# The recurrence at the end of a hybrid attention kernel: 32x32 squares turned by VectorE, and the residual added by GpSimd

## The reference, cut to what matters

```
x = x + window_attention(group_norm(x))                  # layer 0
t = tokens(x)                                            # (16, 3136, 128)
t = t + linear_attention(layer_norm(t))
# the last part:
Wx = layer_norm(t) @ W.T ; Wx = batch_norm(Wx) * gamma + beta
def step(yt, wx_t):
    yt = sigmoid(wx_t + yt @ V.T)
    return yt, yt
ys = scan(step, 0, Wx over the 3136 time steps)          # for each of 16 images
out = t + ys
```

## Time and profile before

| | us |
|---|---|
| median of three runs (1854.69, 1854.74, 1855.60) | 1854.74 |
| span of the profiled execution | 1848.6 |
| what lies around the span, median less span | 6.1 |
| window attention up to about | 787 |
| linear attention, from there to about | 1565 |
| twelve warming steps | 1570.2 to 1585.3 |
| 196 kept steps | 1585.3 to 1840.9 |
| agreement test, last stores and end | 1840.9 to 1848.6 |

### The profile page before, as it was taken

One profiled execution on the slowest core, in us unless ns is written; L12 is line 12 of the kernel. 1 busy time (PEld: TensorE's weight loads), 2 busy tenths in 40 slices (PEclk: granted clock), 3 DMA queues, 4 the chain that ended last, 5 costly groups with the idle time before them and its releaser, 6 DMA issues.

```text
span 1848.6 us, 57765 instructions
## 1 busy us (share of the span) xinstructions
PE 1821.1 (99%) x19624; PEld 1615.1 (87%) x19624; DVE 1523.8 (82%) x4706; ACT 1214.1 (66%) x3179; POOL 1009.8 (55%) x1177
## 2 busy tenths in 40 slices
PE   7999999999999999899999999999999999999998
PEld 6888888888888888799999999999999998888886
DVE  7888888888888888788888888888888887566665
ACT  5777778877787877666666666666666665333333
POOL 6878888888888888633333333333333334432321
PEclk9999999999999999999999999999999999999999
DMA  5333333333333332122222222222223222656543
GB/s 169 102 104 107 107 107 105 105 103 103 105 107 107 107 85 80 47 70 74 66 69 68 67 68 67 70 65 70 64 70 91 70 68 74 222 183 218 190 166 127
DMA packets 207108, 187.02 MB, mean 101 GB/s; under 512 B 14576, under 2 KB 190944, under 8 KB 206816
## 3 DMA queue, kind: packets, MB, share of 16 engines
q1 hardware_dynamic: 205664, 182.14, 32.9%
q10 hardware_dynamic: 1152, 1.13, 0.2%
HBM read 105.95 MB, written 77.27 MB: 99 GB/s over the span
## 4 chain that ended last, share of the span: by engine, by line
PE 54%; issue 27%; POOL 16%; DVE 1%; DMA 1%; POOLq 0%; ACT 0%; ACTq 0%; DVEq 0%; SPq 0%
POOL la_rstd L999 11%; PE k_psum L346 7%; PE k_psum L296 6%; PE k_psum L289 6%; PE k_psum L314 6%; PE k_psum L330 5%; PE k_psum L362 5%; PE k_psum L1425 5%; PE k_psum L1416 5%; PE k_psum L280 4%; POOL la_spread L993 3%; PE k_psum L1406 2%; PE k_psum L1433 2%; POOL la_tn L1004 2%; POOLq L39 0%
## 5 line engine op out<-in xcount | busy, mean ns | idle before, releaser
L993 POOL TENSOR_SCALAR la_spread<-la_mv 128x4 f32<-128x4 f32 (+1 forms) x203 | 45.8, 226 | 477.9 <-DVE la_mv L1103 477.8
L615 POOL TENSOR_TENSOR wa_prob<-wa_prob,wa_peak 128x784 f32<-128x784 f32 x128 | 194.6, 1521 | 117.3 <-DVE wa_peak L481 117.3
L940 ACT ACTIVATE la_ve<-k_psum 128x256 f32<-128x256 f32 x196 | 75.4, 385 | 232.5 <-PE k_psum L821 232.5
L999 POOL TENSOR_TENSOR la_rstd<-la_spread,k_exponent 128x4 f32<-128x4 f32 (+1 forms) x203 | 207.5, 1022 | 17.2 <-POOL la_spread L993 0.4
L1490 ACT ACTIVATE sc_y<-k_psum,sc_cols 128x256 f32<-128x256 f32 x207 | 98.0, 473 | 177.0 <-PE k_psum L1425 177.0
L809 PE MATMUL k_psum<-la_uT,la_wt 128*128 128x256 f32 x784 | 201.9, 380 | 0.0
L622 POOL TENSOR_TENSOR wa_prob<-wa_prob,wa_inv 128x784 f32<-128x784 f32 x128 | 195.0, 1523 | 11.3 <-DVE wa_inv L442 11.3
L1059 DVE SCALAR_TENSOR_TENSOR la_fqk<-k_psum,la_raised 128x512 f32<-128x512 f32 x196 | 135.6, 692 | 74.8 <-ACT la_raised L932 74.6
L1214 POOL TENSOR_TENSOR sc_ub<-sc_tb 128x3584 f32<-128x3584 f32 (+6 forms) x22 | 92.8, 4222 | 172.6 <-PE k_psum L1406 171.3
L473 DVE TENSOR_TENSOR wa_prob<-k_psum,wa_bias 128x784 f32<-128x784 f32 x128 | 125.0, 976 | 66.2 <-PE k_psum L314 66.1
L932 ACT ACTIVATE la_raised<-k_psum,la_minus_one 128x512 f32<-128x512 f32 x196 | 134.7, 687 | 43.3 <-PE k_psum L809 43.1
(11 more groups left out here) (138 smaller groups left out, 5299.5 us busy)
## 6 DMA issues: line engine op xcount, KB each, us to landing
t<-la_tn SPq DMA_DIRECT2D x196, 129.0 KB, 2.2
la_xc<-x SPq DMA_DIRECT2D x196, 128.0 KB, 2.1
wa_xT<-in_x_cm SPq DMA_DIRECT2D x124, 196.0 KB, 3.3
sc_tb<-t SPq DMA_DIRECT2D x12, 1806.0 KB, 8.1
out<-sc_ob SPq DMA_DIRECT2D x12, 1792.0 KB, 12.1
wa_xw<-in_x_tok SPq DMA_DIRECT2D x64, 224.0 KB, 2.7
wa_xw<-in_x_tok SPq DMA_DIRECT2D x64, 168.0 KB, 2.3
x<-wa_y SPq DMA_DIRECT2D x64, 168.0 KB, 2.8
```

Of the source, the lines that this page charges most:

```text
L615: nc.gpsimd.tensor_tensor(s, s, peak[:, k % S, :].unsqueeze(2).broadcast_to([128, PAIRS * HEADS, WIN]), ALU.subtract).then_inc(lowered, 1)
L999: nc.gpsimd.tensor_tensor(rstd[:, n % S, used], spread[:, used], exponent[:, used], ALU.pow).then_inc(rooted, 1)
```

## The change

t2 gets another layout: (128, 196 steps, 8 blocks, 33). Partition p = 32 q + c holds channels 32 q to 32 q + 31 of the columns c, 32 + c, 64 + c, ..., and behind each 32 channels stands the reciprocal deviation. So a step's 128 x 256 numbers consist of 4 x 8 squares of 32x32, and turning each square in place puts channels on the partitions. VectorE does this, SBUF to SBUF, for two steps in one instruction. Linear attention writes the rows of `tn` in this layout: each token's row becomes four pieces of 33 numbers, and a store is cut wherever a segment ends. `tn` holds four pieces of 33.

In the scan, the two matmuls of a step are split into two halves of 128 columns, with semaphores and PSUM banks of their own. `uT` has four buffers of two steps, `y` three, `ob` three tiles. Most tiles have 10 steps for 14. The residual is added by GpSimd in one instruction for each tile, in place in `ob`; only for the last two tiles (4 and 2 steps) does VectorE do it. The output is written in the squares' layout and put in order on the host. Of the columns, 7 of 8 blocks are loaded early, for 3 of 4 half groups before.

```
-        EARLY = 3 * UNITS // 4
+        EARLY = -(-EARLY_BLOCKS * SQ * STEPS // (2 * P))
...
                     sp.wait_ge(tabled, n + 1)
-                    sp.dma_start(rows(t2, n), tn[:, n % XS]).then_inc(stored[n % XS], 16)
+                    for a, p, q, col, s in pieces(n):
+                        dst = bass.AP(t2.tensor, ((col % SQ * STEPS + s) * NB + col // SQ) * SF,
+                                      [[NB * SF, q - p], [SQ * STEPS * NB * SF, QUADS], [1, SF]])
+                        sp.dma_start(dst, tn[p:q, n % XS, a]).then_inc(stored[n % XS], 16)
...
+MAIN_PLAN = [(0, 4, True), (4, 8, True)] + [(12 + 10 * j, 10, True) for j in range(17)] + [(182, 8, True), (190, 4, True), (194, 2, True)]
+KEPT_TILES = 3
+U_PAIRS = 4
+Y_PAIRS = 3
+EARLY_BLOCKS = 7
...
+        for j in range(TILES + 4):
+            if inside(j - 4, TILES) and j - 4 >= FIRST:
+                store(j - 4)
+            if inside(j, TILES):
+                load(j)
...
+        def residual(j):
+            if not inside(j, TILES) or not by_pool(j):
+                return
+            pool.wait_ge(y_turned, pairs_to[j] + by_pool(j) - WARM_PAIRS)
+            size = 2 * by_pool(j)
+            kept = ob[:, slot(j), 0:size, :].rearrange("p s (b r) -> p s b r", b=NB)
+            nc.gpsimd.tensor_tensor(kept, kept, tb[:, j % 4, 0:size, :, 0:SQ], ALU.add).then_inc(pool_summed, 1)
+
+        for j in range(TILES + 2):
+            scale(j)
+            residual(j - 2)
...
+        for t in range(-1, NT):
+            for h in range(2):
+                state_part(t, h)
+                input_part(t + 1, h)
...
+        def turn_tokens(p):
+            if not inside(p, PAIRS):
+                return
+            j, i = where[p]
+            dve.wait_ge(u_made, j + 1)
+            at_least(dve, w_done, 4 * (p - U_PAIRS + 1))
+            nc.vector.transpose(uT[:, p % U_PAIRS].rearrange("p s c -> p (s c)"),
+                                ub[:, j % 2, i:i + 2].rearrange("p s b r -> p (s b r)")).then_inc(u_turned, 1)
...
+        def turn_states(p):
+            if not inside(p, PAIRS) or p < WARM_PAIRS:
+                return
+            j, i = where[p]
+            for h in range(2):
+                dve.wait_ge(y_made[h], 2 * p + 2)
+            at_least(dve, stored[slot(j)], stores(j))
+            states = y[:, p % Y_PAIRS].rearrange("p s c -> p (s c)")
+            if i < 2 * by_pool(j):
+                nc.vector.transpose(ob[:, slot(j), i:i + 2, :].rearrange("p s c -> p (s c)"), states).then_inc(y_turned, 1)
+            else:
+                nc.vector.transpose(b_y[p % 2], states).then_inc(y_turned, 1)
...
+        for p in range(-3, PAIRS + 1):
+            hand(p)
+            turn_states(p - 1)
...
+            turn_tokens(p + 3)
+            residual(p - 1)
```

More of the change, by code:

```diff
@@ L716, in rows, with quads, pieces, stores_through @@
             return dram.rearrange("b t c -> (b t) c")[n * 2 * P:(n + 1) * 2 * P, :].rearrange("(a p) c -> p a c", p=P)
+        def quads(tile):
+            return tile.rearrange("p (q r) -> p q r", q=QUADS)
+        def pieces(n):
+            found = []
+            for a in range(2):
+                first = (2 * n + a) * P
+                token = first
+                while token < first + P:
+                    upto = min(first + P, (token // STEPS + 1) * STEPS)
+                    found.append((a, token - first, upto - first, token // STEPS, token % STEPS))
+                    token = upto
+            return found
+        def stores_through(k, units):
+            return 16 * sum(len(pieces(m)) for m in range(k, units, XS))
         def quotient_bank(n):
@@ L1302, in _ @@
             link(nc.vector.tensor_copy(flag[:, :], flag_f[:, :]))
-            nc.vector.tensor_copy(self.final[:, :], self.tiles["y"][:, (WARM + STEPS - 1) % 2, :])
+            nc.vector.tensor_copy(self.final[:, :], self.state(WARM + STEPS - 1))
         @block.tensor
@@ new lines, in scan, with by_pool @@
+    b_state = [[bank[2 * h + i] for i in range(2)] for h in range(2)]
+    b_y = bank[4:6]
+    TILES = len(plan)
+    where = [(j, i) for j in range(TILES) for i in range(0, plan[j][1], 2)]
+    PAIRS = len(where)
+    NT = 2 * PAIRS
+    FIRST = sum(not kept for _, _, kept in plan)
+    pairs_to = [sum(size for _, size, _ in plan[0:j]) // 2 for j in range(TILES + 1)]
+    WARM_PAIRS = pairs_to[FIRST]
+    WARMED = 2 * WARM_PAIRS
+    def by_pool(j):
+        return plan[j][1] // 2 if FIRST <= j < TILES - 2 else 0
@@ new lines, in loads, with stores, pool_sums, vector_sums @@
+    def loads(j):
+        return 16 * sum(2 if i < FIRST else 1 for i in range(j % 4, j + 1, 4))
+    def stores(j):
+        return 16 * len(range(FIRST + (j - FIRST) % KEPT_TILES, j, KEPT_TILES))
+    def pool_sums(j):
+        return sum(by_pool(i) > 0 for i in range(FIRST, j))
+    def vector_sums(j):
+        return sum(plan[i][1] // 2 - by_pool(i) for i in range(FIRST, j))
+    def slot(j):
+        return (j - FIRST) % KEPT_TILES
+    def half(h):
+        return slice(h * HALF, (h + 1) * HALF)
@@ L1397, in _, with input_part @@
     @block.tensor
     def _(pe):
[L1399 to L1409 removed]
+        def input_part(t, h):
             if not inside(t, NT):
@@ new lines, in residual @@
+        def residual(p):
+            if not inside(p, PAIRS) or p < WARM_PAIRS:
+                return
+            j, i = where[p]
+            if i < 2 * by_pool(j):
+                return
+            dve.wait_ge(y_turned, p - WARM_PAIRS + 1)
+            nc.vector.tensor_tensor(ob[:, slot(j), i:i + 2, :].rearrange("p s (b r) -> p (s b) r", b=NB),
+                                    b_y[p % 2].rearrange("p (s r) -> p s r", r=SQ),
+                                    tb[:, j % 4, i:i + 2, :, 0:SQ].rearrange("p s b r -> p (s b) r"), ALU.add).then_inc(summed, 1)
```

216 lines of the change are left out of this document (86 added, 130 removed).

## The result

The changed kernel takes **1783.69 us** (median of four runs, 1783.15 to 1784.31) where the kernel before, run beside it, takes 1855.17 (1854.69 to 1855.97): a ratio of 0.9618, 95% interval 0.9604 to 0.9631, 71.5 us less. The forecast was 1800 (1780 to 1838): the sign and the range held, the forecast gain was 16 us too small, and the engine that was to bound the kernel (GpSimd) does not.

A forecast was written before the change was run, and what follows sets the result against it. GpSimd was to bound the recurrence at 1.05 us a step: 56 us less there, +1.5 us at the start, -55 (rounded) in sum; 1854.7 - 55 = 1800 us, range 1780 to 1838.

The forecast's parts named there:

- rival 4: Recurrence: GpSimd's add is as cheap as its scaling, so the 0.95 us loop binds; 1786 us, chance 0.10.
- TensorE after the change: Recurrence: with the turning moved to VectorE, four products of 0.215 us are left, 0.86 us a step.
- The loop of a half: Recurrence, state to state for 128 columns: product 0.485, sigmoid 0.367, gaps 0.04 and 0.06, together 0.95 us.
- VectorE's turns: Recurrence: two turns of 512 elements for two steps, 0.69 us each, hidden; upper bound 1.22 us each.
- GpSimd is the bound: Recurrence: scaling 4.6 us and residual add 5.9 us a tile of 10 steps, 10.5 together, 1.05 us a step.
- The recurrence to the span's end: From the first step: GpSimd ends at 211 us, stores at 218, span at 222, against 278.4 before.
- The start: Start of the recurrence: more store issues, smaller packets, a squares' turn for PE's turn and copy; +1.5 us, bounds -1 and +6.
- The loads just in time: SP's queue in the recurrence: load behind a tile's store lands in about 10 us, within GpSimd's 10.5 us.
- The middle stage hides: Linear attention's 132 B stores: 7 to 28 ns a packet, at 28 ns 2.2 of a unit's 3.98 us with loads.
- Rival 1: Middle stage: the 132 B stores bind from 55 ns a packet; at 70 ns 1988 us, slower; chance 0.18.
- rival 2: Middle-stage stores: some DMA engines carry far more packets; at 42 ns 1900 us; chance 0.07, within the 0.18 for binding stores.
- Stores under 512 bytes: Middle-stage stores: read, changed and written back per the skill page; at twice the row's price 55 ns, right at the edge.

## Why the prediction was right, and where it was not

The sign came from the right place, TensorE's turns and the halved loop. That the time lies within the range is in part luck: the range had been drawn to take in rival 4, to which the forecast gave 0.10, and the mechanism of the forecast itself, GpSimd as the bound, did not happen.

- **TensorE after the change** (0.86 us forecast): 0.89 by the starts. Right.
- **The loop of a half** (0.95): 0.944 to 0.953. Right, and the number that decides the time.
- **VectorE's turns** (0.69 us each; two passes 1.22): 0.670 and 0.711. The lower bound was the right choice; VectorE hides with room for all the adds.
- **GpSimd is the bound, 10.5 us a tile, 1.05 us a step**: this is the step that failed. It had two terms. The penalty for runs of 32, 0.17 us each way, is not there. The add, sized at 2.16 ns an element from two adds with 384 and 512 elements, goes at 1.96 (5177 ns for 2560, 2167 for 1024). The Trainium skill, GPSIMD Engine Reference, Elementwise — side-by-side cycle accounting, gives 4497 ns for an add of 2048 elements; the one of 2048 here took 4169 (mean of two), so the page errs to the same side as my rows. So 9.64 us, or 9.54 by the starts, replaces 10.5. That is level with the next limit, the loop at 9.5, and the run without the add shows that the loop sets the time. Rival 4 (the loop binds, 1786 us, chance 0.10) is what happened, though not for its reason: the add is dearer than the scaling, 5.18 to 4.46 us, and still cheap enough. And the runs without the add show that even a load of 98% needs a test before it is called a bound.
- **The recurrence to the span's end** (222 us): 209.5 (1573.0 to 1782.5). GpSimd's last add ends 198 us after the first step, where its sum had 211. The tail's place was right (stores behind GpSimd's last add); it is 11.3 us from the last state to the span's end, 2.1 of them from that add.
- **The start** (+1.5): +2.9, and part of it was in no term: 1.3 us are there already when linear attention ends, and TensorE, idle for 3 us, starts at half clock. With the gap filled the recurrence is 0.9 us shorter.
- **The loads just in time**: GpSimd's scalings waited 1.8 us for them in all. Right.
- **The middle stage hides** (7 to 28 ns a packet): 14.7 ns, unit 3.98 us, landing 3.0 us for 2.1. Right for this kernel. The distance was wrong: the edge was put at 55 ns a packet, nearly four times what the packet takes, while 20% more packets already bring it (256 on 1331 cost 14 us). The threshold was worked out from the time that one packet occupies an engine, with the packets spread evenly and one behind the other; that time does not stay as it is under load (31 ns in the mean), and single packets are held up. Nothing in the forecast's sum stood for this. Rival 1 was nearer than its 0.18 looks.
- **Uneven shares** (rival 2): they cost nothing visible here, as the unit kept its 3.98 us. How near to the edge they bring the kernel is not shown. The Trainium skill, DMA: Bandwidth & Descriptors, on why a DMA increments its semaphore by 16, would by my count put 100 packets on each of four engines; adding the second copy in equal shares was cheaper by 59 us of 388 than adding it in such pieces.
- **Stores under 512 bytes** (the same page, Specifications: read, changed, written back): had it doubled the row's price, the packet would take 55 ns; 14.7 were measured, against 28 for a row before the change. No run here shows whether the memory reads first.
- **The sum**: -55 forecast, -66 in the span, -71.5 in the time. 11 of the missing 16.5 us are in the span (the recurrence to the span's end 12.5 too high, the start 1.4 too low). The rest lies around it: the forecast kept the 6.1 us of a median over one short span, where this kernel has 1.7 to 1.9.

## What to carry to other kernels

Where two limits stand side by side (here 1.30 and 1.27 us a step), remove both or expect little: one edit gave 0 us, the other 9, the two together 71.5. An engine that is 98% busy may just be keeping up; leave its work out once before tuning it. And for small packets, add a fifth and then two fifths more of them on purpose: neither the share of busy time nor the time of one packet shows how near the edge is.

## What the runs showed of the hardware that was not expected

- Small stores: the loop of loads and 132-byte stores on one queue stopped at about 385 packets a us in the mean over 100 us (381 to 392 in four kernels), with a busy share between 50 and 82%, although 1172 packets went through in one us of the same trace. The median time of a packet stayed at 14 ns while the mean went from 14.7 to 31.
- TensorE's clock: with one of the two products of a half cut to a quarter, the granted clock stayed at 1.2 GHz for the whole recurrence, and the kernel took 155 us more than the changed one. In the changed kernel, after an idle stretch of 3 us ahead of the recurrence, it ran 3 us at 1.2 GHz and then rose to 2.4.
- VectorE's instructions in a row overlap: three with durations of 2.05 us in all start over again every 1.89 us.
- A turn of the 32x32 squares of 512 columns costs VectorE what a two-input operation of 512 does (0.67 to 0.71 us; 692 ns in the earlier trace rows), and short runs of 32 cost GpSimd nothing.
